# Row maxima of neighbouring PSUM banks taken in pairs by VectorE, in the attention stage of a fused cross-attention and expert kernel

## The chip, the cores and the metric

One core of a Trainium2 chip runs the whole program. The metric is the device time of one execution in microseconds (us). The engines are TensorE (PE in the profile, with its weight loads as PEld), VectorE (DVE), ScalarE (ACT), GpSimd (POOL) and the DMA queues, most of them fed by SyncE (SP). PSUM has eight banks; a bank holds 512 fp32 numbers in each of 128 partitions.

## The reference, cut to what matters

```python
# B=4, S=512, D=256, 16 heads of 16; ctx has the shape of x
q = split(layernorm(x) @ Wq + bq); k = split(ctx @ Wk + bk); v = split(ctx @ Wv + bv)
scores = einsum('bhqd,bhkd->bhqk', q, k) / sqrt(16)
p = softmax(scores, axis=-1)
x = x + einsum('bhqk,bhkd->bhqd', p, v).merge_heads() @ Wo + bo
y = layernorm(x); yn = rmsnorm(y) * norm_w
sim = per head and half: (yn @ wq) . keys            # 8 heads, 2 halves, 64 keys
s1, s2 = top 16 of each half; choose the top 16 of the 256 sums
hidden = gelu(yn . expert_down[chosen]) * relu(score)
x = x + sum(hidden * expert_up[chosen])
```

Softmax subtracts the largest score of a row (one query of one head). Finding these largest scores is what the change touches.

## The kernel before

The attention runs in 16 **groups** of four heads (`NG = 16`, four groups for each of the four batch entries). A group has 16 **blocks** (steps `i = 0..15`): head `i // 4` of the group, and 128 queries `i % 4`, against all 512 keys. Block number `n = 16 g + i` runs through all groups.

The scores are computed twice. `scores(g, i)` (line 1501) multiplies a block with the queries in the partitions into bank `n % 3`, one of **three** banks; VectorE reduces it to one negated maximum for each query (line 1293). When a group's 16 blocks are reduced, `max_parts(g)` (lines 1102 to 1106) splits the maxima into two bf16 parts, TensorE turns them (event "max" at step 3 of the next group), ScalarE copies them out, and SyncE relays them through DRAM into two extra rows of the group's query tile. Two groups later `turned_scores(g, i)` (line 1511) multiplies the same scores turned, with the maxima already subtracted by the two extra rows, into bank 3 or 4; ScalarE exponentiates them (`probabilities`, line 984), and `values` multiplies four blocks of them with the values (four fp32 matmuls into bank 5, at steps 1, 5, 9 and 13).

So in the slot of group g, TensorE does for each step i, in this order: the planned events of the step (transposes and projections for other parts of the program, all through banks 6 and 7), the turned scores of group g - 2, the scores of group g, and at `i % 4 == 1` the values. The order on every engine is fixed by these loops; engines meet at semaphores:

```python
if n >= 3:
    pe.wait_ge(s_max, n - 2)        # scores: block n-3 is reduced
if n >= 2:
    pe.wait_ge(p_ready, n - 1)      # turned scores: its bank is exponentiated
dve.wait_ge(s_full, n + 1)          # reduction: block n is multiplied
```

VectorE's loop has, for each step: at step 0 `max_parts` of the last group, then the reduction of the step, then whatever else is placed there: `first_norm` at step 3 and `first_norm_apply` at step 8 (first group of a batch entry), `normalise` at step 4, residual and second norm at steps 12 to 15 of every fourth group, and from group 8 on the **tasks** of the expert choice (`choose_experts`): 17 tasks for each tile of 128 tokens, spread over two groups from step 5 of the even one. A task is a search (8 top-8 steps and their bookkeeping), a choice, the making of keys or an extraction, of one to three microseconds. In even groups from 8 on, TensorE has two events "sim" at steps 2 and 6, fp32 matmuls of 512 columns.

After the attention, from about 440 us, the experts' stage follows, in which nothing is changed.

## Time and profile before

| | |
|---|---|
| median of 3 runs | 1168.51 us (1166.11 to 1168.63) |
| the profiled execution | 1168.72 us |
| its span, first to last instruction | 1166.9 us |
| TensorE busy | 1032.4 us (88%) |
| VectorE busy | 943.8 us (81%) |
| ScalarE busy | 393.6 us (34%) |
| GpSimd busy | 636.7 us (55%) |
| mean granted TensorE clock | 0.942 of full speed |

Busy shares are means over stages with different limits, so they don't say which engine sets the time of one stage; the views by stretch do. An engine's busy time counts the duration of its instructions, and on VectorE an instruction may start a little before the duration of the one ahead has ended. Several instructions of one line in a row are merged into one row of the timeline (x4). A matmul's end is modelled. In the rows, `mem` is the one SBUF tensor that holds all tiles, and `bank` a PSUM bank.

### The profile page before, as it was taken

To read this page: it belongs to the slowest core of one execution; us is meant where nothing else is said; L and a number is where in the kernel's file an instruction comes from. 1 tells how busy PE (TensorE), PEld (TensorE's weight loads), DVE (VectorE), ACT (ScalarE), POOL (GpSimd) and SP (SyncE) were. 2 spreads that over 40 slices of the span, in tenths; PEclk is the share of its full clock that TensorE was granted. 3 is DMA by queue.
4 is the path that set the end of the run, shared out by engine and by line. 5 is a ranking of instruction groups with operands and counts; after the bars stand their busy time and mean duration, and the time that the engine had idled before them with its cause. 6 is when DMAs were issued, how large, how long until landed. Compare 5 with 4: busy or idle time off the path is not lost.

```text
span 1166.9 us, 28159 instructions
## 1 busy us (share of the span) xinstructions
PE 1032.4 (88%) x10088; PEld 722.1 (62%) x10088; DVE 943.8 (81%) x4847; ACT 393.6 (34%) x725; POOL 636.7 (55%) x793
## 2 busy tenths in 40 slices
PE   5899989876778686598989989999999999999998
PEld 3434444233213224577878778887888878888887
DVE  3676557989998999899999899999989999943210
ACT  2266645443444362232222222222222222222211
POOL 6330510532122225686787777878877787776511
PEclk9799989998969798699999999999999999999999
DMA  7534324222111103700000000000000000000000
GB/s 204 141 131 135 111 74 141 65 92 87 52 51 43 51 7 108 280 3 12 17 21 21 22 21 17 27 11 27 27 15 22 22 17 25 27 31 2 2 19 10
DMA packets 60347, 63.82 MB, mean 55 GB/s; under 512 B 7184, under 2 KB 56592, under 8 KB 59696
## 3 DMA queue, kind: packets, MB, share of 16 engines
q1 hardware_dynamic: 59728, 61.63, 16.6%
q8 instruction: 80, 1.31, 0.5%
q10 hardware_dynamic: 480, 0.39, 0.2%
q14 instruction: 59, 0.48, 0.1%
HBM read 42.34 MB, written 19.66 MB: 53 GB/s over the span
## 4 chain that ended last, share of the span: by engine, by line
PE 42%; DVE 33%; POOL 11%; issue 7%; ACT 2%; DMA 2%; SPq 1%; ACTq 0%; DVEq 0%; POOLq 0%
PE bank L1383 39%; POOL mem L863 4%; DVE mem L1293 4%; DVE mem L1338 4%; PE bank L1386 3%; DVE mem L1229 3%; DVE mem L1176 2%; DVE mem L1175 2%; DVE mem L1225 2%; DVE mem L1232 2%; DVE mem L1212 1%; DVE mem L1335 1%; POOL mem L724 1%; POOL mem L870 1%; DVE mem L1180 1%
## 5 line engine op out<-in xcount | busy, mean ns | idle before, releaser
L1383 PE MATMUL bank<-mem 128*128 128x32 bf16 (+6 forms) x9608 | 984.2, 275 | 93.8 <-DVE mem L1293 34.5
L1383 PEld LDWEIGHTS bank<-mem 128*128 128x128 bf16 (+4 forms) x9608 | 669.8, 122 | 363.0 <-issue 161.4
L863 POOL TENSOR_TENSOR mem<-mem 128x1536 bf16<-128x1536 bf16 x123 | 340.8, 2772 | 138.3 <-DVE mem L1335 138.1
L1293 DVE TENSOR_REDUCE mem<-bank 128x1 f32<-128x512 f32 x256 | 167.8, 682 | 59.8 <-PE bank L1383 58.9
L984 ACT ACTIVATE mem<-bank 128x512 f32<-128x512 f32 x256 | 147.8, 602 | 183.8 <-PE bank L1383 183.0
L1338 DVE TENSOR_TENSOR mem<-mem,bank 128x2048 bf16<-128x2048 bf16 x128 | 155.3, 1213 | 0.0
L1040 ACT COPY mem<-bank 128x512 f32<-128x512 f32 x128 | 75.1, 586 | 113.9 <-PE bank L1383 113.9
L870 POOL TENSOR_TENSOR mem<-mem 128x512 f32<-128x512 f32 x64 | 83.3, 1302 | 50.5 <-ACT mem L1029 50.5
L1386 PE MATMUL bank<-mem 128*128 128x128 f32 (+3 forms) x480 | 74.7, 287 | 37.4 <-DVE mem L1093 11.4
L1386 PEld LDWEIGHTS bank<-mem 128*128 128x128 f32 (+3 forms) x480 | 55.1, 141 | 78.2 <-issue 46.1
L724 POOL TENSOR_TENSOR mem<-mem 128x32 f32<-128x32 f32 (+5 forms) x224 | 45.8, 244 | 97.5 <-DVE mem L1184 97.5
L1031 ACT ACTIVATE bank<-bank 128x512 f32<-128x512 f32 x64 | 37.2, 582 | 171.3 <-PE bank L1383 171.3
L1029 ACT ACTIVATE mem<-bank 128x512 f32<-128x512 f32 x64 | 38.3, 599 | 161.3 <-PE bank L1383 161.3
L1335 DVE TENSOR_TENSOR mem<-mem,bank 128x512 bf16<-128x512 bf16 x128 | 52.3, 409 | 47.6 <-PE bank L1383 44.2
L1352 DVE TENSOR_TENSOR mem<-bank,mem 128x512 f32<-128x512 f32 x64 | 43.8, 684 | 47.0 <-ACT bank L1031 39.0
L1175 DVE FIND_INDEX8 mem<-mem 128x8 uint32<-128x64 f32 x256 | 52.9, 219 | 0.0
L1176 DVE MATCH_REPLACE8 mem<-mem 128x64 f32<-128x64 f32 x256 | 51.6, 209 | 0.0
L745 POOL TENSOR_TENSOR mem<-mem 128x128 f32<-128x128 f32 x16 | 7.2, 451 | 72.8 <-DVE mem L1246 72.8
L1229 DVE MATCH_REPLACE8 mem<-mem 128x50 f32<-128x50 f32 x256 | 46.9, 194 | 0.0
L1180 DVE MAX8 mem<-mem 128x8 f32<-128x64 f32 x256 | 44.2, 215 | 0.0
L1172 DVE MAX8 mem<-mem 128x8 f32<-128x64 f32 x256 | 43.5, 211 | 0.0
L759 POOL TENSOR_SCALAR mem<-mem 128x4 f32<-128x4 f32 x4 | 0.9, 237 | 65.4 <-DVE mem L1085 65.3
(105 smaller groups left out, 770.5 us busy)
## 6 DMA issues: line engine op xcount, KB each, us to landing
mem<-parts_d SPq DMA_DIRECT2D x186, 64.0 KB, 2.3
parts_d<-mem SPq DMA_DIRECT2D x16, 384.0 KB, 3.0
mem<-in_L_ffn_expert_down SPq DMA_DIRECT2D x16, 256.0 KB, 2.8
downT_d<-mem SPq DMA_DIRECT2D x16, 256.0 KB, 3.0
mem<-downT_d SPq DMA_DIRECT2D x4, 1024.0 KB, 7.9
mem<-in_L_ffn_expert_up SPq DMA_DIRECT2D x4, 1024.0 KB, 10.9
tok_d<-mem SPq DMA_DIRECT2D x16, 160.0 KB, 1.8
mem<-tok_d SPq DMA_DIRECT2D x16, 160.0 KB, 2.4
```

The costliest lines, as they stand in the source:

```text
L863: nc.gpsimd.tensor_tensor(ow[q % 2], i0, i1, ALU.mult).then_inc(ow_rdy, 1)
L870: nc.gpsimd.tensor_tensor(gm[q % 4], gm[q % 4], coef[par][:, 2 * q:2 * q + 2, :], ALU.mult)\
L984: nc.scalar.activation(p_sb[quad % 3][:, hh, :], psum[3 + n % 2][:, :], ACT.Exp, scale=DK ** -0.5)\
L1040: nc.scalar.copy(coef[1 - par][:, :, q * TK:(q + 1) * TK], src).then_inc(c_ev, 1)
L1175: steps.count(nc.vector.max_index(i[:, h, c, 0:8], s[:, h, c, 0:8], src[c]))
L1176: cut = [steps.count(nc.vector.match_replace(left[c], s[:, h, c, 0:8], src[c], GONE)) for c in range(2)]
L1229: b.append(steps.count(nc.vector.match_replace(k[:, h, :], o[:, h, 0:8], k[:, h, :], 0.0)))
L1293: nc.vector.tensor_reduce(nmx[g % 2][:, i % TB, i // TB:i // TB + 1], psum[n % 3][:, :], AX.X, ALU.max, negate=True).then_inc(s_max, 1)
L1335: nc.vector.tensor_tensor(oj[q % 2], low.to_broadcast([P, TP, JL, PAIR]), numbers[:, 0:JL, :].unsqueeze(1).to_broadcast([P, TP, JL, PAIR]) ...
L1338: nc.vector.tensor_tensor(oh[q % 2], high.to_broadcast([P, TP, P, PAIR]), numbers.unsqueeze(1).to_broadcast([P, TP, P, PAIR]), ALU.is_equa ...
L1383: return nc.tensor.matmul(o, l, r, start=first, stop=last)
L1386: return nc.tensor.transpose(o, i, ident)
```

## The change

The three banks of the scores become one PSUM tensor of three banks, `bank012`, so that one instruction can read two neighbouring ones. `neighbours(g)` decides for each group which steps are reduced together: two blocks in banks 0 and 1, or in banks 1 and 2 where a group begins at bank 1, and never across the end of a group. A pair is reduced by one instruction at the step of its second block, after the wait for that block, and raises `s_max` by two when it ends. Blocks in bank 2, and those left over, are reduced alone as before. A group that begins at bank 1 has six pairs and four single blocks, any other five pairs and six single blocks. The maxima in `nmx` now lie head by head, as the blocks come, and `max_parts` reads them turned round. TensorE's, ScalarE's and the queues' code is the same.

```diff
-        psum = [ctx.enter_context(nc.psum_tensor(f"bank{i}", [P, 512], F32)) for i in range(8)]
+        three = ctx.enter_context(nc.psum_tensor("bank012", [P, 3 * 512], F32)).rearrange("p (i t) -> p i t", i=3)
+        psum = [three[:, i, :] for i in range(3)]
+        psum += [ctx.enter_context(nc.psum_tensor(f"bank{i}", [P, 512], F32)) for i in range(3, 8)]
...
-        nmx = [mem.take(TB * HG).rearrange("p (t h) -> p t h", t=TB) for _ in range(2)]
+        nmx = [mem.take(HG * TB) for _ in range(2)]
...
+        def neighbours(g):
+
+            last, i = {}, 0
+            while i < 16:
+                blocks = 2 if (16 * g + i) % 3 < 2 and i < 15 else 1
+                i += blocks
+                last[i - 1] = blocks
+            return last
+
+        reduced = [neighbours(g) for g in range(NG)]
...
-                m, n = mpart[g % 2], nmx[g % 2]
+                m, n = mpart[g % 2], nmx[g % 2].rearrange("p (h t) -> p t h", h=HG)
...
-                    if g < NG:
-                        n = 16 * g + i
+                    if g < NG and i in reduced[g]:
+                        n, blocks = 16 * g + i, reduced[g][i]
                         dve.wait_ge(s_full, n + 1)
-                        nc.vector.tensor_reduce(nmx[g % 2][:, i % TB, i // TB:i // TB + 1], psum[n % 3][:, :], AX.X,
-                                                ALU.max, negate=True).then_inc(s_max, 1)
+                        nc.vector.tensor_reduce(nmx[g % 2][:, i + 1 - blocks:i + 1], three[:, n % 3 + 1 - blocks:n % 3 + 1, :],
+                                                AX.X, ALU.max, negate=True).then_inc(s_max, blocks)
```

What stands in a row on an engine is shown at two stretches of the program. The first is group 4, which begins at bank 1. On VectorE before, from block 3 of the group to block 8 (BN_STATS and BN_AGGR are `first_norm`, RECIPROCAL and TENSOR_TENSOR `normalise`):

```order
L1293 TENSOR_REDUCE mem<-bank1 128x1 [waits s_full]
L1080 BN_STATS mem<-mem 128x6 [waits x_ld2]
L1080 BN_STATS mem<-mem 128x6 x3
L1085 BN_AGGR mem<-mem 128x2 [waits ln_stat,ln_rstd]
L1085 BN_AGGR mem<-mem 128x2 [waits ln_stat] x3
L1293 TENSOR_REDUCE mem<-bank2 128x1 [waits s_full]
L1116 RECIPROCAL mem<-bank7 128x16 [waits misc_read1,misc_full1]
L1120 TENSOR_TENSOR mem<-bank7,mem 128x4x64 [waits nrm]
L1293 TENSOR_REDUCE mem<-bank0 128x1 [waits s_full]
L1293 TENSOR_REDUCE mem<-bank1 128x1 [waits s_full]
L1293 TENSOR_REDUCE mem<-bank2 128x1 [waits s_full]
L1293 TENSOR_REDUCE mem<-bank0 128x1 [waits s_full]
```

On VectorE now, from the pairs of blocks 0, 1 and 2, 3 to block 7 (`128x2` is a pair) and `first_norm_apply` (TENSOR_SCALAR):

```order
L1306 TENSOR_REDUCE mem<-bank012 128x2 [waits s_full] x2
L1093 BN_STATS mem<-mem 128x6 [waits x_ld2]
L1093 BN_STATS mem<-mem 128x6 x3
L1098 BN_AGGR mem<-mem 128x2 [waits ln_stat,ln_rstd]
L1098 BN_AGGR mem<-mem 128x2 [waits ln_stat] x3
L1306 TENSOR_REDUCE mem<-bank012 128x1 [waits s_full]
L1129 RECIPROCAL mem<-bank7 128x16 [waits misc_read1,misc_full1]
L1133 TENSOR_TENSOR mem<-bank7,mem 128x4x64 [waits nrm]
L1306 TENSOR_REDUCE mem<-bank012 128x2 [waits s_full]
L1306 TENSOR_REDUCE mem<-bank012 128x1 [waits s_full]
L1106 TENSOR_SCALAR mem<-mem 128x256 [waits misc_full0,ln_stat,ln_rstd]
L1106 TENSOR_SCALAR mem<-mem 128x256 x3
```

Blocks 2 and 3, 5 and 6, 8 and 9 are one instruction each, at the place of the second; the other work of the steps keeps its place.

On TensorE before, group 4 from step 6 to step 9 (bank 3 or 4 with `p_ready` is a turned score, a wait for `s_max` a score, 128x128 transposes of an event):

```order
L1383 MATMUL bank3<-mem 128x512 [waits p_ready]
L1383 MATMUL bank1<-mem 128x512 [waits s_max]
L1386 MATMUL bank6<-mem 128x128 [waits dn_ld0,misc_read0]
L1386 MATMUL bank6<-mem 128x128 x3
L1383 MATMUL bank4<-mem 128x512 [waits p_ready]
L1383 MATMUL bank2<-mem 128x512 [waits s_max]
L1383 MATMUL bank3<-mem 128x512 [waits p_ready]
L1383 MATMUL bank0<-mem 128x512 [waits s_max]
L1386 MATMUL bank7<-mem 128x128 [waits wq_ld0,misc_read1]
L1386 MATMUL bank7<-mem 128x128 x3
L1383 MATMUL bank4<-mem 128x512 [waits p_ready]
L1383 MATMUL bank1<-mem 128x512 [waits s_max]
```

Nothing moved there; the same rows stand there now, with `bank012` for banks 0 to 2. But the scores of step 8 (the third row that waits for `s_max`) need block 5, which VectorE now reduces together with block 6.

The other stretch is the end of group 13 and the start of group 14. On VectorE before, from block 13 of group 13 (MAX with 128x50, MATCH_REPLACE are an extraction, the rest down to the CAST the decoding of a tile, then `max_parts`):

```order
L1293 TENSOR_REDUCE mem<-bank2 128x1 [waits s_full]
L1293 TENSOR_REDUCE mem<-bank0 128x1 [waits s_full]
L1225 MAX mem<-mem 128x8 x4
L1229 MATCH_REPLACE mem<-mem 128x50 [waits dve_step] x4
L1232 MAX mem<-mem 128x8 [waits dve_step] x4
L1241 TENSOR_SCALAR mem<-mem 128x128 [waits dve_step,misc_full1,wsp]
L1243 TENSOR_SCALAR mem<-mem 128x128
L1244 TENSOR_SCALAR mem<-mem 128x128
L1246 SCALAR_TENSOR_TENSOR mem<-mem 128x128 [waits dve_step]
L1249 CAST mem<-mem 128x128 [waits dve_step]
L1250 CAST mem<-mem 128x128
L1293 TENSOR_REDUCE mem<-bank1 128x1 [waits s_full]
```

On VectorE now, from the single block 13 to the pair of blocks 14 and 15:

```order
L1306 TENSOR_REDUCE mem<-bank012 128x1 [waits s_full]
L1238 MAX mem<-mem 128x8 x4
L1242 MATCH_REPLACE mem<-mem 128x50 [waits dve_step] x4
L1245 MAX mem<-mem 128x8 [waits dve_step] x4
L1254 TENSOR_SCALAR mem<-mem 128x128 [waits dve_step,misc_full1,wsp]
L1256 TENSOR_SCALAR mem<-mem 128x128
L1257 TENSOR_SCALAR mem<-mem 128x128
L1259 SCALAR_TENSOR_TENSOR mem<-mem 128x128 [waits dve_step]
L1262 CAST mem<-mem 128x128 [waits dve_step]
L1263 CAST mem<-mem 128x128
L1306 TENSOR_REDUCE mem<-bank012 128x2 [waits s_full]
```

The reduction of block 14 has moved behind the extraction and the decoding, to that of block 15.

## Rows read from the trace of the kernel before

**Rows 1.** The page's groups, and the line alone with its first and last start

```profile
L1293 DVE TENSOR_REDUCE mem<-bank 128x1 f32<-128x512 f32 x256 | 167.8, 682 | 59.8 <-PE bank L1383 58.9
...
L1293 DVE TENSOR_REDUCE mem<-bank x256: 655/680/693, 31.8 to 412.0; 128x1 f32<-128x512 f32 x128
```

**Rows 2.** Busy us by stretch: columns PE, PEld, DVE, ACT, POOL, clock, DMA

```profile
31.00:76.00 45.00, 41.56 (x183) 20.48 (x183) 34.56 (x69) 19.67 (x38) 18.05 (x22) 0.83 0.46 138
76.00:188.00 112.00, 104.80 (x568) 47.46 (x568) 66.64 (x134) 66.19 (x137) 23.01 (x36) 0.95 0.38 119
188.00:412.00 224.00, 174.18 (x764) 63.54 (x761) 210.85 (x1218) 99.25 (x192) 59.52 (x161) 0.86 0.20 64
```

**Rows 3.** Chain by line, from 76 to 188 us, then from 188 to 412

```profile
by line: PE bank L1383 67.8%; PE bank L1386 12.8%; issue 4.9%; ACT mem L937 1.4%; POOL mem L787 1.3%; POOL mem L795 1.3%; ACT mem L992 1.3%; ACT mem L984 1.2%; DVE mem L1129 1.2%; DVE mem L1133 1.1%; DVE mem L1149 0.9%; ACT mem L915 0.6%; D
...
by line: DVE mem L1293 19.7%; PE bank L1383 15.1%; issue 4.8%; DVE mem L1175 3.6%; DVE mem L1176 3.6%; DVE mem L1229 3.2%; SPq L508 2.8%; PE bank L1386 2.5%; DVE mem L1180 2.4%; DVE mem L1172 2.4%; DVE mem L1184 2.1%; DVE mem L1232 2.0%; DV
```

**Rows 4.** Waits from 76 to 188 us: us in total, times, longest

```profile
DVE mem L1293 <- PE bank L1383: 39.4, 40, 3.0
```

**Rows 5.** Waits from 188 to 412 us

```profile
PE bank L1383 <- DVE mem L1293: 32.0, 27, 2.2
...
DVE mem L1293 <- PE bank L1383: 9.7, 13, 1.9
```

**Rows 6.** Timeline (start, us, what), the relay before group 3

```profile
75.96 0.39 PE L1383 MATMUL bank<-mem 98*128 98x512 bf16 x1 [1.59 <-DMA mem<-mrow_d]
```

**Rows 7.** Timeline, VectorE, a run of reductions and two short ones

```profile
102.82 2.47 DVE L1293 TENSOR_REDUCE mem<-bank 128x1 f32<-128x512 f32 x4
...
184.24 0.17 DVE L1102 CAST mem<-mem 128x16 bf16<-128x16 f32 x1
```

**Rows 8.** Timeline, matmul to reduction, and reduction to matmul

```profile
170.83 0.38 PE L1383 MATMUL bank<-mem 96*128 96x512 bf16 x1
...
171.25 0.69 DVE L1293 TENSOR_REDUCE mem<-bank 128x1 f32<-128x512 f32 x1 [0.96 <-PE bank L1383]
...
268.11 0.68 DVE L1293 TENSOR_REDUCE mem<-bank 128x1 f32<-128x512 f32 x1
...
268.85 0.61 PE L1383 MATMUL bank<-mem 96*128 96x512 bf16 x1 [1.46 <-DVE mem L1293]
```

**Rows 9.** Timeline, late places: reduction of the second block, TensorE two blocks on

```profile
84.67 0.69 DVE L1293 TENSOR_REDUCE mem<-bank 128x1 f32<-128x512 f32 x1 [0.18 <-PE bank L1383]
...
85.34 0.60 PE L1383 MATMUL bank<-mem 98*128 98x512 bf16 x2
...
103.32 0.63 PE L1383 MATMUL bank<-mem 98*128 98x512 bf16 x2
...
183.51 0.69 DVE L1293 TENSOR_REDUCE mem<-bank 128x1 f32<-128x512 f32 x1 [0.58 <-PE bank L1383]
...
183.95 0.61 PE L1383 MATMUL bank<-mem 98*128 98x512 bf16 x2
```

**Rows 10.** Timeline, VectorE and TensorE from group 13 to group 14

```profile
348.64 1.27 DVE L1293 TENSOR_REDUCE mem<-bank 128x1 f32<-128x512 f32 x2
...
352.55 0.68 DVE L1293 TENSOR_REDUCE mem<-bank 128x1 f32<-128x512 f32 x1
...
355.49 0.69 DVE L1293 TENSOR_REDUCE mem<-bank 128x1 f32<-128x512 f32 x1 [0.36 <-PE bank L1383]
...
349.45 6.00 PE L1383 MATMUL bank<-mem 96*128 96x512 bf16 x17 [0.38 <-DVE mem L1293]
...
349.83 1.06 PE L1383 MATMUL bank<-mem 98*128 98x512 bf16 x2
```

**Rows 11.** Timeline, VectorE's waits at three reductions

```profile
187.94 0.69 DVE L1293 TENSOR_REDUCE mem<-bank 128x1 f32<-128x512 f32 x1 [1.92 <-PE bank L1383]
...
365.99 0.69 DVE L1293 TENSOR_REDUCE mem<-bank 128x1 f32<-128x512 f32 x1 [1.20 <-PE bank L1383]
...
254.58 0.69 DVE L1293 TENSOR_REDUCE mem<-bank 128x1 f32<-128x512 f32 x1 [1.20 <-PE bank L1383]
```

## The prediction

> **What bounds the kernel now.** I read the views in the order of the groups above. The page [rows 1] gives the instruction at stake: 256 row-maximum reductions of 0.682 us, 167.8 us of VectorE, with 59.8 us of VectorE idling ahead of them, nearly all spent waiting for TensorE. All lie between 31 and 412 us. The busy time by stretch [rows 2] splits that time in two. From 76 to 188 us (groups 3 to 7 of the 16) TensorE is busy 104.80 of 112 us and VectorE only 66.64: TensorE sets the pace. From 188 to 412 us (groups 8 to 15, with the choice of experts on VectorE) it is the reverse: VectorE 210.85 of 224 us, TensorE 174.18. The chain by line agrees [rows 3]: in the first stretch 67.8% and 12.8% of it are TensorE lines and the reduction is not named; in the second the reduction leads with 19.7%. The waits say what could be gained: in the first stretch VectorE waits 39.4 us for scores [rows 4], so a cheaper reduction buys nothing there; in the second TensorE waits for the reduction (32.0 us in 27 waits) and VectorE for TensorE in only 13 places, 9.7 us [rows 5]. Before 76 us the end of the chain is a relay through DRAM: TensorE starts group 3 at 75.96 us after a wait of 1.59 us for it [rows 6]. After 412 us nothing that the change touches is left, and what is gained or lost by then passes on one to one.
>
> **What the change removes.** By the rule that picks pairs, a group has five or six, 85 in all: 171 instructions instead of 256. Groups 8 to 15 have 42 pairs (two groups of six, six of five), groups 3 to 7 have 27. What a pair saves: four reductions in a row take 2.47 us and the last one of them 0.68, so they start (2.47 - 0.68) / 3 = 0.597 us apart [rows 7]. The time per element I take from two VectorE rows of different length, 16 elements in 0.17 us and 512 in 0.68: 0.51 / 496 = 1.03 ns, 0.53 us for 512. So a pair lasts 0.68 + 0.53 = 1.21 us and the next instruction starts 1.13 us after it, against 1.194 for two: 0.064 us saved. The other bound is the whole fixed part of an instruction's duration, 0.68 - 0.53 = 0.15 us. I take 0.064, since start to start is what a busy engine pays. Where VectorE is the bound that is 42 x 0.064 = 2.7 us **gained**; in groups 3 to 7 nothing is.
> The Trainium skill (VectorE: DVE Perf Modes, section "The TRN2 errata — SBUF-src ops pay a fixed extra latency per instruction") gives 120 cycles fixed for a PSUM source and says that many small tiles pay it each: by that, an estimate from the page, the 42 pairs would save 42 x 0.125 = 5.3 us instead of 2.7, and the sum below would be 2.6 us less. The trace shows such a fixed time in the duration, but not between starts; it is rival C below.
> That the maxima now lie head by head makes the first cast and the subtraction of `max_parts` read with a stride; 16 elements in 0.17 us [rows 7], once a group: nothing, 0.1 us each at most.
>
> **What it adds: a bank comes free later.** TensorE may write scores n+3 only when block n is reduced. With a pair (n, n+1) the bank of n waits for block n+1 to be multiplied, and for 1.21 us instead of 0.68. The links [rows 8]: a reduction starts 0.42 us after its matmul (170.83 to 171.25), and a matmul that waited for a bank starts 0.06 us after the reduction's end (268.11 + 0.68 = 268.79 to 268.85). So a pair whose second block's reduction began at R before lets TensorE write two blocks further on at R + 1.21 + 0.06 at the earliest. Compare with when it did so before [rows 9]: a row "x2" is a turned-score matmul and a score matmul, the score starting 0.38 us before the row's end.
> Group 4, blocks 5 and 6: R = 102.82, because VectorE is kept until then by another task (blocks 5 to 8 are the four in a row of [rows 7]); new release 104.09. Block 8's matmul started at 103.32 + 0.63 - 0.38 = 103.57: 0.53 us late. Blocks 6 and 7 of group 3: 84.67 + 1.27 = 85.94 against 85.34 + 0.60 - 0.38 = 85.56: 0.38 us. Last pair of group 7: 183.51 + 1.27 = 184.78 against 184.18: 0.60 us. What decides is what TensorE has between the second block and the second next: with the values' four fp32 matmuls there, the release is in time; with only transposes or nothing, it is not. Over groups 3 to 7 there are seven late places, the first, the one above and the last shown: two at 0.38 us, four at 0.60, one at 0.53. The other 20 pairs are covered by the values, projections or waits for other buffers. TensorE's stream behind the seven is dense (busy 104.80 of 112 us), and behind the waiting matmul on its queue stand the turned scores, the values and the transposes, so ScalarE's exponentials slip with it. Sum: 0.76 + 2.40 + 0.53 = 3.7 us **lost**. Bounds: 0 if waits for ScalarE absorb it all, 5 if the second bank of a cycle is late too.
> In groups 0 to 2 the same happens, but group 3 waits for the relay [rows 6]; 1.59 us cover it. I cost it at nothing; with that cover used up it is 0.5 us.
>
> **The stretch that VectorE bounds.** There the task of the first block (a search, a choice) now runs before the pair, so the bank of the first block comes free a task and a reduction later. Mostly TensorE has room (it waits 32.0 us there anyway). Not at the start of group 14, the place of the third excerpt. Blocks 13 and 14 of group 13 were reduced back to back from 348.64, the second done at 349.91 [rows 10]; TensorE wrote group 14's block 1 at once (349.83 + 1.06 - 0.63 = 350.26) and then ran its stream of 6.00 us (values, both similarity matmuls) that ends with block 2, for which VectorE waited 0.36 us at 355.49. Now block 14 is reduced with block 15, behind the extraction and the decoding, ending at 352.55 + 0.68 - 0.06 = 353.17; block 1's matmul starts at 353.23 instead of 350.26, and the stream behind it ends 3.0 us later with VectorE idle: **3.0 us lost**. Groups 8, 10 and 12 end in other phases and keep their release.
> Where VectorE waited for the second block of a pair [rows 11], it had done the first in the meantime; now it does both after the wait. Three places: 187.94 (followed by another wait, 0.17 us and dense work: 0.3 us), one in group 12 and 365.99 (0.53 each): 1.4 us lost. The wait of 1.20 us at 254.58 is for the first block of one; now a search of 1.7 us runs in it: 0.9 us gained (0 to 1.20). Sum for this stretch: -2.7 + 3.0 + 1.4 - 0.9 = +0.8; bounds -3.6 (nothing late) and +4.5 (another place like group 14's half as dear).
>
> **Sum.** The profiled execution took 1168.72 us (span 1166.9 and what lies around it), 0.2 over the median of 1168.51. 1168.7 + 3.7 + 0.8 = 1173.2; I forecast **1173.2 us**.
>
> **Rivals.**
> *A, slower still by the clock.* TensorE runs at half clock in stretches: mean 0.95 from 76 to 188 us, 0.86 from 188 to 412 [rows 2]. Seven more gaps could add such stretches. If 0.95 becomes 0.92, the first stretch takes 112 x (0.95 / 0.92 - 1) = 3.7 us more: 1176.9. Against it: the gaps are only 0.4 to 0.6 us, and the mean in the second stretch, where TensorE already waits in 27 places and more, is still 0.86.
> The Trainium skill (TensorE: Matmul & The Clock Gate, section "A second HAM failure mode: psum-queue depth-cycling") tells of this very thing, short idles between groups of matmuls that cycle through PSUM making the clock fall and rise; the means of the two stretches are in line with it, but do not show the cause.
> *B, absorbed.* TensorE also waits for ScalarE; if those waits swallow the seven stalls: 1168.7 + 0.8 = 1169.5, no change. Against it: in the two rows of [rows 9] TensorE goes on without a gap.
> *C, the whole fixed part is saved.* 0.15 instead of 0.064 us in 42 pairs is 3.6 us more: 1173.2 - 3.6 = 1169.6, no change. For it: nothing but the durations.
> *D, the other side: three banks are deep enough everywhere.* VectorE paces the scores in all groups, TensorE catches up within a group, and every pair pays out: 85 x 0.064 = 5.4 us, 1163.3. It decides if TensorE has 0.6 us to spare behind each late bank; 104.80 busy of 112 us speaks against it.
> That the pairs are not formed is ruled out by the excerpts.
>
> **How the numbers follow.** Forecast (1171 to 1175.5) 0.50; A 0.22; B 0.12; C 0.08; D 0.08. Slower by over 0.2% (2.3 us, about what a measurement of this kernel can tell from no change): forecast and A, 0.72. Within: B and C, 0.20. Faster: D, 0.08. The range, 1169.0 to 1179.0, takes in A, B and C but not D nor A's far end.
>
> **What would show it.** In the changed kernel's profile: 85 rows of about 1.21 us with two outputs and 86 of 0.68; VectorE's busy time less by 85 x 0.15 = 13 us of row time though little is gained; group 8's first maxima about 3.7 us later than before, each late place a wait of TensorE for the reduction just before a score matmul; from there to the last maximum (412.0 before) another 0.8 us, with one VectorE wait of over 3 us early in group 14 and the idle time at 254.58 gone; the time after the last maximum unchanged. I am wrong if a pair is much shorter than 1.21 us, if the first stretch does not lengthen, or if the granted clock in either stretch moves by more than 0.02.

## The result, and the profile after

| | before | after |
|---|---|---|
| median | 1168.63 us (5 runs, 1166.11 to 1170.39) | 1177.14 us (5 runs, 1176.61 to 1181.81) |
| ratio, 95% interval | | 1.0086 (1.0062 to 1.0111) |
| the profiled execution, its span | 1168.72, 1166.9 us | 1176.61, 1174.8 us |
| VectorE busy, its instructions | 943.8 us, 4847 | 938.2 us, 4762 |
| TensorE busy | 1032.4 us | 1030.0 us |
| mean granted TensorE clock | 0.942 | 0.944 |

Slower by 0.86% by the ratio of the runs (the two medians differ by 8.5 us, 0.73%); the forecast was slower, by 0.4% (1173.2 us), the range 1169.0 to 1179.0. VectorE has 85 instructions fewer and 5.6 us less to do, and the kernel takes 8.5 us more at the medians.

The reduction in the profile after: the page's row of the line, and the line by shape. It answers to [rows 1]:

```profile
L1306 DVE TENSOR_REDUCE mem<-bank 128x1 f32<-128x512 f32 (+1 forms) x171 | 159.0, 948 | 74.7 <-PE bank L1396 74.6
...
L1306 DVE TENSOR_REDUCE mem<-bank 128x2 f32<-128x1024 f32 x85 | 103.6, 1218 | 66.3 <-PE bank L1396 66.3
L1306 DVE TENSOR_REDUCE mem<-bank 128x1 f32<-128x512 f32 x86 | 58.5, 681 | 8.4 <-PE bank L1396 8.3
```

85 pairs of 1.218 us and 86 singles of 0.681. The idle time ahead of the reductions rose from 59.8 to 74.7 us, and nearly all of it now stands ahead of pairs, since a pair waits for its second block.

The busy time of the two stretches, each taken to the same point of the program as in [rows 2] (columns as there):

```profile
76.00:191.00 115.00, 104.00 (x570) 47.98 (x568) 65.56 (x111) 67.40 (x139) 23.01 (x36) 0.99 0.37 117
191.00:421.00 230.00, 174.31 (x762) 64.28 (x760) 209.12 (x1178) 99.21 (x191) 59.90 (x162) 0.86 0.20 62
```

The first stretch is 3 us longer with 104.00 us of TensorE's work as before, although its clock was even higher (0.99 against 0.95); the second is 6 us longer. The waits for the reduction in the two, which answer to [rows 4, 5]:

```profile
DVE mem L1306 <- PE bank L1396: 44.8, 30, 3.7
...
PE bank L1396 <- DVE mem L1306: 4.7, 10, 0.9
...
PE bank L1396 <- DVE mem L1306: 42.7, 31, 4.9
...
DVE mem L1306 <- PE bank L1396: 18.2, 13, 5.4
```

In the first stretch TensorE's matmuls waited for the reduction in 10 places, 4.7 us; before, in 2, 1.4 us. In the second they waited 42.7 us instead of 32.0, and VectorE for TensorE 18.2 us instead of 9.7, **in 13 places again**. One of those is 5.41 us long; it is the start of group 14:

```profile
350.91 0.67 DVE L1306 TENSOR_REDUCE mem<-bank 128x1 f32<-128x512 f32 x1
...
354.22 1.22 DVE L1306 TENSOR_REDUCE mem<-bank 128x2 f32<-128x1024 f32 x1
...
362.29 1.82 DVE L1306 TENSOR_REDUCE mem<-bank 128x2 f32<-128x1024 f32 x2 [5.41 <-PE bank L1396]
...
355.49 6.69 PE L1396 MATMUL bank<-mem 96*128 96x512 bf16 x15 [3.17 <-DVE mem L1306]
```

These are rows of VectorE's and, the last one, of TensorE's timeline; they answer to [rows 10]. The single block 13 of group 13 is reduced at 350.91. Block 14 could be, too, but stands with block 15 at 354.22, behind the extraction and the decoding. TensorE waits 3.17 us for its bank, runs the stream of values and similarities that was 4.8 us long before and is 6.3 now, and VectorE waits 5.41 us for the block at its end.

To compare runs, I use **slots**: the time from the first instruction of `max_parts` for one group (the cast, L1102, L1115 or L1117) to that of the next, so the slot of group g is that in which its own scores are reduced. The slot of group 14 before, and after:

```profile
353.26 0.27 DVE L1102 CAST mem<-mem 128x16 bf16<-128x16 f32 x1
...
385.53 0.17 DVE L1102 CAST mem<-mem 128x16 bf16<-128x16 f32 x1
```

```profile
355.47 0.17 DVE L1115 CAST mem<-mem 128x16 bf16<-128x16 f32 x1
...
393.91 0.17 DVE L1115 CAST mem<-mem 128x16 bf16<-128x16 f32 x1
```

385.53 - 353.26 = 32.3 us before, 393.91 - 355.47 = 38.4 us after. All slots that matter, taken in the same way from each trace (group 10 stands apart, see below; "to the end" is from the last cast to the last turned score matmul):

| kernel | groups 1 to 7 | 8 | 9 | 10 | 11 | 12 | 13 | 14 | 15 | to the end |
|---|---|---|---|---|---|---|---|---|---|---|
| before | 136.4 | 27.9 | 28.9 | 33.1 | 27.2 | 24.7 | 27.2 | 32.3 | 27.2 | 25.7 |
| after | 139.6 | 28.3 | 28.3 | 32.6 | 26.9 | 25.4 | 27.0 | 38.4 | 27.4 | 24.3 |

Two numbers carry the result: +3.2 us up to group 7, and +6.1 in the slot of group 14. The rest of groups 8 to 15 with the end is 1.7 us **shorter** than before, but 1.4 us of that lies behind the last cast, where nothing is reduced any more. The busy time of that stretch before, and after, columns as in [rows 2]:

```profile
412.70:438.50 25.80, 20.83 (x106) 5.78 (x106) 23.41 (x197) 17.30 (x33) 6.98 (x27) 0.93 0.02 8
```

```profile
421.30:445.70 24.40, 19.38 (x107) 5.51 (x106) 22.39 (x191) 18.09 (x34) 6.93 (x27) 1.00 0.03 8
```

TensorE needs 19.38 instead of 20.83 us there, at a granted clock of 1.00 instead of 0.93. The slots of groups 8 to 13 and 15 together are only 0.3 us shorter.

### The profile page after: what moved, and what is told of

It is laid out like the page before. It is cut to its first block, busy times and chain, and to the rows that moved or that the text cites. A ratio compares the mean times of both kernels' runs of the same rounds, so it can differ in the third digit from the quotient of the medians.

```text
span 1174.8 us, 28159 instructions
## 1 busy us (share of the span) xinstructions
PE 1030.0 (88%) x10088; PEld 723.5 (62%) x10088; DVE 938.2 (80%) x4762; ACT 394.1 (34%) x725; POOL 636.8 (54%) x793
## 4 chain that ended last, share of the span: by engine, by line
PE 43%; DVE 34%; POOL 11%; issue 7%; ACT 2%; DMA 2%; SPq 1%; ACTq 0%; DVEq 0%; POOLq 0%
PE bank L1396 40%; DVE mem L1306 5%; DVE mem L1351 4%; POOL mem L876 4%; PE bank L1399 3%; DVE mem L1242 2%; DVE mem L1189 2%; DVE mem L1188 2%; DVE mem L1238 2%; DVE mem L1245 1%; DVE mem L1225 1%; DVE mem L1348 1%; DVE mem L1193 1%; DVE mem L1185 1%; POOL mem L737 1%
## 5 line engine op out<-in xcount | busy, mean ns | idle before, releaser
L1306 DVE TENSOR_REDUCE mem<-bank 128x1 f32<-128x512 f32 (+1 forms) x171 | 159.0, 948 | 74.7 <-PE bank L1396 74.6
```

The source lines that it names most:

```text
L1306: nc.vector.tensor_reduce(nmx[g % 2][:, i + 1 - blocks:i + 1], three[:, n % 3 + 1 - blocks:n % 3 + 1, :], AX.X, ALU.max, negate=True).then ...
```

## The experiments

Theory T: the change costs at few places, where a score bank comes free late and TensorE has nothing else to do; elsewhere it saves a little. Its rivals: E, every pair costs a little (8.5 / 85 = 0.1 us) by the two-bank read itself; A, what is lost in the first stretch is absorbed behind it (this is B of the prediction; the letters here are those of the expectations); K, the granted clock, by which no edit of single pairs would make a definite change. All kernels of a group ran on one chip beside the kernel before, whose median was 1167.24, 1168.5 and 1167.63 us for the three groups.

### Which pairs cost: one undone, those from group 8, those up to group 7

```diff
-                blocks = 2 if (16 * g + i) % 3 < 2 and i < 15 else 1
+                blocks = 2 if (16 * g + i) % 3 < 2 and i < 15 and (g, i) != (13, 14) else 1
```

> The changed kernel with one pair undone: blocks 14 and 15 of group 13 are reduced one by one, block 14 again ahead of the extraction and the decoding; the other 84 pairs stay. Theory T (few late banks): the step from 2.3 to 6.7 us that the traces show at the start of group 14 goes; 4 to 6 us less than the changed kernel, that is 1171 to 1173 us, +0.3% to +0.4% on the kernel before; score matmuls of group 14 from block 2 on are 2 to 3 us later than before instead of 6.7. Rival E (every pair costs about 8 / 85 = 0.1 us, by the two-bank read itself): 0.1 us less, 1177 us. Rival K (the granted clock): no definite change.

```diff
+                blocks = 2 if (16 * g + i) % 3 < 2 and i < 15 and g >= 8 else 1
```

> Pairs only in groups 8 to 15 (42), groups 0 to 7 as before. Theory T: group 8 starts as in the kernel before (within 0.3 us instead of 2.9 later); the rest keeps its loss, so about 3 us less than the changed kernel, 1174 us, with the step at group 14. Rival E: 43 x 0.1 = 4.3 us less, 1173 us, and the delay grows evenly through groups 8 to 15 instead of in steps.

```diff
+                blocks = 2 if (16 * g + i) % 3 < 2 and i < 15 and g < 8 else 1
```

> Pairs only in groups 0 to 7 (43), the rest as before. Theory T: group 8 starts 2.5 to 3.2 us later than in the kernel before, in steps of 0.4 to 1.0 us at single blocks of groups 3 to 7, and that delay is carried to the end: 1171.5 us. Rival E: 1173 us, evenly grown. Rival A (absorbed by what VectorE bounds behind it): less than 1 us at the end, 1169.5.

| pairs | ratio to before, 95% | groups 1 to 7 | 8 | 9 | 10 | 11 | 12 | 13 | 14 | 15 | to the end |
|---|---|---|---|---|---|---|---|---|---|---|---|
| all but one | 1.0051 (1.0032 to 1.0069) | 140.0 | 28.3 | 28.3 | 32.8 | 26.9 | 25.4 | 26.9 | 31.6 | 27.3 | 24.3 |
| from group 8 | 1.0047 (1.0034 to 1.0061) | 136.6 | 28.0 | 29.7 | 35.0 | 26.9 | 25.5 | 27.0 | 36.5 | 27.3 | 24.3 |
| to group 7 | 1.0043 (1.0025 to 1.0061) | 140.2 | 28.0 | 29.2 | 31.8 | 27.2 | 24.7 | 27.2 | 32.0 | 27.4 | 25.5 |

Groups 1 to 7 take 139.6 to 140.2 us with pairs in them and 136.4 to 136.6 without, whatever stands behind. It isn't given back later: with pairs up to group 7 alone the program is 5.0 us slower at the medians, so rival A falls. With one pair of 85 undone, the slot of group 14 falls to 31.6 us, and its block 2 is multiplied 0.06 us after the cast (1.82 before, 6.33 in the changed kernel). So rival E falls: 84 pairs are left and that slot has its old length. Against the kernel before the program is now 0.51% slower instead of 0.86% (0.69% in a repeat below); the intervals of these overlap, and the same pair is tested twice more below. The two halves lose 0.47% and 0.43%, 0.90% together, against 0.86% and 0.69% for the whole; the intervals allow it.

### The order without the merging

```diff
-                        nc.vector.tensor_reduce(nmx[g % 2][:, i + 1 - blocks:i + 1], three[:, n % 3 + 1 - blocks:n % 3 + 1, :],
-                                                AX.X, ALU.max, negate=True).then_inc(s_max, blocks)
+                        for back_by in range(blocks - 1, -1, -1):
+                            nc.vector.tensor_reduce(nmx[g % 2][:, i - back_by:i - back_by + 1], psum[n % 3 - back_by], AX.X,
+                                                    ALU.max, negate=True).then_inc(s_max, 1)
```

> All pairs keep their place in VectorE's order (both reductions at the step of the second block), but are two instructions of one bank each, each raising the semaphore by one. It parts the order from the merging. Theory T: in groups 3 to 7 the first bank comes free 0.5 to 0.6 us earlier than with the merged one, and the late places all but go: group 8 starts within 0.6 us of the kernel before. At the start of group 14 the bank still waits behind the extraction: 3.5 to 5 us lost there. The 42 merged savings of 0.06 us go too (2.7 us). Sum 1168.6 + 0.5 + 2.7 + 5 = 1176.8, 1175 to 1178 us: about the changed kernel's time, but with the loss all behind 188 us. Rival E (the two-bank read costs): about the kernel before, 1168.6 us.

1174.66 us, ratio 1.0058 (1.0039 to 1.0076), so most of the loss is there without a merged instruction. The expected 1176.8 us counts 2.7 us for savings that "go too", but the kernel before, from which that sum starts, never had them; without them it is 1174.1. Its profiled execution was the quickest of its nine (1167.90 us, the others 1170.26 to 1177.35), so its trace tells where single places wait, not what makes up the median: the slot of group 14 is 3.6 us longer in it, the median some 7 us, and the difference stays open. The waits of TensorE's matmuls for the reduction in the first stretch, of this kernel, and of the one with pairs up to group 7 (us, times, longest):

```profile
PE bank L1397 <- DVE mem L1307: 0.9, 2, 0.5
```

```profile
PE bank L1396 <- DVE mem L1306: 4.7, 10, 0.9
```

0.9 us in 2 places against 4.7 in 10: the late places of the first stretch come from the **merging**, since the first of two single reductions frees its bank 0.54 us earlier than a merged one (0.68 against 1.22 us after their start). From group 3's step 4 to group 8's step 1 it takes 102.1 us, as kernels with the old order there do (102.1 to 102.8), against 105.7 to 106.1 with the pairs. The slot of group 14 is 35.9 us here: most of what is lost there comes from the **order**. And this run prices the merged instruction where VectorE is the bound: the slot of group 11 is 27.2 us with single reductions in either order and 26.9 with five pairs: 0.3 / 5 = 0.06 us for a pair.

### One pair alone

```diff
+                blocks = 2 if (g, i) == (13, 14) else 1
```

> The kernel before with a single pair, blocks 14 and 15 of group 13. Theory T: that pair alone makes the score matmul of group 14, block 1, 3.0 us late, and the slot of group 14 (from its maxima's split to the next one's) 35.5 to 37.5 us instead of 32.0 to 32.7; total 3 to 5 us over the kernel before, nothing else moves by more than the clock's phase. Rival E (many pairs each cost a little): 0.1 us, no difference.

1172.42 us, ratio 1.0042 (1.0024 to 1.0060): 4.8 us by **one** merged instruction out of 255. Groups 1 to 7 take 136.4 us as before, groups 8, 9, 11, 12, 13 and 15 are within 0.1 us of before, group 10 is at 33.8 and the end at 25.3; the slot of group 14 is 37.4 us instead of 32.3. Its rows, VectorE and then TensorE:

```profile
348.88 0.68 DVE L1306 TENSOR_REDUCE mem<-bank 128x1 f32<-128x512 f32 x1
...
352.20 1.22 DVE L1306 TENSOR_REDUCE mem<-bank 128x2 f32<-128x1024 f32 x1
...
360.24 0.69 DVE L1306 TENSOR_REDUCE mem<-bank 128x1 f32<-128x512 f32 x1 [4.78 <-PE bank L1396]
...
353.47 6.73 PE L1396 MATMUL bank<-mem 96*128 96x512 bf16 x15 [2.75 <-DVE mem L1306]
```

The same picture with nothing else changed: the pair at 352.20, TensorE 2.75 us idle before block 1's matmul at 353.47, and VectorE 4.78 us idle for the end of the stream. For comparison, the kernel with pairs from group 8 on but without this one (below), where TensorE starts after 0.32 us and the whole run of 17 is 4.25 us long:

```profile
348.90 1.27 DVE L1306 TENSOR_REDUCE mem<-bank 128x1 f32<-128x512 f32 x2
...
352.81 0.68 DVE L1306 TENSOR_REDUCE mem<-bank 128x1 f32<-128x512 f32 x1
...
349.72 4.25 PE L1396 MATMUL bank<-mem 96*128 96x512 bf16 x17 [0.32 <-DVE mem L1306]
```

### Pairs where the wait is covered

In the first stretch: pairs only up to group 7, and only where the values stand between the second block and the matmul that needs the first one's bank.

```diff
+                blocks = 2 if (16 * g + i) % 3 < 2 and i < 15 and g < 8 and i % 4 in (0, 3) else 1
```

> Pairs only in groups 0 to 7 and only where the values' four fp32 matmuls stand on TensorE's queue between the second block and the matmul that waits for the first's bank (the second block's step is 0 or 1 modulo 4): 30 pairs of 43. Theory T: no bank is late; from the score matmul of group 3, step 4, to that of group 8, step 1, 102 to 103 us as before instead of 106, and the total within 0.2% of the kernel before. Rival E (each pair costs by itself): 30 / 43 of the 3.3 us, 2.3 us more.

1168.99 us, ratio 1.0007 (0.9989 to 1.0024). TensorE's wait for the reduction there:

```profile
PE bank L1396 <- DVE mem L1306: 0.5, 1, 0.5
```

One place, 0.5 us, and 102.0 us from group 3's step 4 to group 8's step 1, against 102.1 to 102.8 in kernels without pairs there. Groups 1 to 7 even take 134.7 us in this trace, and 135.4 in that of the two single reductions, where slots 1 to 3 together, with the relay, are shorter; I didn't follow that, and no median shows it. So these pairs cost nothing and, with VectorE not the bound, bring nothing; the others hold the loss of that stretch.

In the second stretch: pairs from group 8 on but for the dear one.

```diff
+                blocks = 2 if (16 * g + i) % 3 < 2 and i < 15 and g >= 8 and (g, i) != (13, 14) else 1
```

> Pairs only in groups 8 to 15, at the step of the second block as in the changed kernel, but blocks 14 and 15 of group 13 apart: 41 pairs. Theory T: no late bank in groups 0 to 7, none at the start of group 14; what is left is the saving of the merged instruction less the waits for second blocks: 1 to 2 us faster than the kernel before, 0.1%. Rival (the release behind a task costs in other places too): 0.2% slower or more.

1168.25 us, ratio 1.0008 (0.9991 to 1.0024): the same as before, not the 1 to 2 us faster that I expected. Its slots from group 8: 28.0, 28.8, 33.7, 26.9, 25.4, 27.0, 31.6, 27.4 and 24.3 to the end, without group 10 219.4 against 221.1 before: 1.7 us gained in the trace, too little for the medians to show. And 1.4 of these stand behind the last cast, at a clock of 1.00 against 0.93 as in the changed kernel; in the slots themselves, group 10 again left out, 41 pairs gained 0.3 us.

### Pairs at the first block's place

If the loss is the bank that waits behind a task, a pair may be reduced at the step of its first block, with the task behind it.

```diff
-            last, i = {}, 0
+            first, i = {}, 0
             while i < 16:
-                blocks = 2 if (16 * g + i) % 3 < 2 and i < 15 else 1
+                blocks = 2 if (16 * g + i) % 3 < 2 and i < 15 and g >= 8 else 1
+                first[i] = blocks
                 i += blocks
-                last[i - 1] = blocks
-            return last
+            return first
...
                         n, blocks = 16 * g + i, reduced[g][i]
-                        dve.wait_ge(s_full, n + 1)
-                        nc.vector.tensor_reduce(nmx[g % 2][:, i + 1 - blocks:i + 1], three[:, n % 3 + 1 - blocks:n % 3 + 1, :],
+                        dve.wait_ge(s_full, n + blocks)
+                        nc.vector.tensor_reduce(nmx[g % 2][:, i:i + blocks], three[:, n % 3:n % 3 + blocks, :],
```

> Pairs only in groups 8 to 15, and reduced at the step of the FIRST block: VectorE waits there for the second block too, and the tasks of the first block run behind the pair instead of ahead of it. Theory T: the first block's bank comes free 0.53 us later than before instead of a task and a reduction later, so the steps at the start of group 14 go. Each pair saves 0.064 us (2.7 us in all), but in 11 of 42 places the second block is not there when VectorE comes to the first, by 0.2 to 2.6 us, 12 us in all, of which it waited about 7 before: 2 to 5 us lost there. Sum: 0 to +2.5 us on the kernel before. Rival (late banks don't matter in this stretch, and the changed kernel lost there by the clock): the same 5.5 us as with pairs at the second block.

And the same with pairs only where, by the trace of before, the second block lay ready at the first one's step, 30 of them:

```diff
+        READY = {8: [7, 10, 13], 9: [0, 9, 12], 10: [0, 12, 14], 11: [1, 4, 7, 10, 13], 12: [0, 9, 12], 13: [0, 2, 5, 8, 11, 14], 14: [10, 13], 15: [0, 3, 7, 9, 12]}
...
-                blocks = 2 if (16 * g + i) % 3 < 2 and i < 15 and g >= 8 else 1
+                blocks = 2 if (16 * g + i) % 3 < 2 and i < 15 and i in READY.get(g, ()) else 1
```

> The same, but only the 30 pairs of groups 8 to 15 whose second block, by the trace of before, is multiplied at least 0.4 us before VectorE comes to the first; all else as in the kernel before. Theory T: 30 x 0.064 = 1.9 us gained, no bank late where it counts: 0.15% faster than the kernel before. If the whole fixed part of 0.15 us were saved: 4.5 us, 0.4% faster. Rival: any two-bank read or any later release costs, 0.2% to 0.4% slower.

1173.9 us, ratio 1.0042 (1.0028 to 1.0055), and 1172.2 us, ratio 1.0025 (1.0012 to 1.0038), where I had expected at most 2.5 us (0.2%) slower for the first and 0.15% faster for the second: two misses, and in the total the first came out about as its rival had it (5.5 us). The slot of group 14 is indeed 32.7 and 31.7 us, so the dear place is gone. But that of group 10 is 36.9 and 36.5, and in the first of the two that of group 12 is 27.0 against 24.7. So I ran the second once more, and the kernel before with it:

> The variant with 30 pairs at the place of their first block once more, for a second trace. Its first trace showed 1.8 us gained outside group 10's slot and 3.4 us lost in it, where TensorE's stream of fp32 matmuls ran at half clock; the unchanged code of groups 8 to 15 took 31.8, 33.1 and 35.7 us there in three traces. Theory P (group 10's slot depends on the phase of the clock, whatever the pairs): the slot is somewhere between 31 and 37 us again, and the total within 0.3% of the kernel before. Theory Q (the early pairs cause it): 36 to 37 us again, and 0.2% to 0.4% slower.

> The kernel before, unchanged, timed against itself, for a second trace of it and for what the comparison makes of no change. Ratio 1.000 within 0.15%. Group 10's slot between 31 and 37 us (33.1 in the first trace); all the others as in the first trace within 0.5 us, but for those in which the granted clock differs.

The early pairs again: ratio 1.0022 (1.0007 to 1.0038), group 10's slot 36.5. The kernel before against itself: 0.9999 (0.9984 to 1.0013), slot 32.8, all other slots within 0.7 us of its first trace. With three traces at 36.5, 36.5 and 36.9 against five in which that stretch is unchanged at 31.8 to 35.7 (33.1, 32.8, 31.8, 33.8 and 35.7), it is likelier that this belongs to the early pairs (theory Q), but the ranges almost meet. What the slot hangs on is TensorE's stream between blocks 1 and 2 of the group. The windows of just that stream, in the kernels with unchanged code there (pairs up to group 7; before again; pairs with the values behind), columns as in [rows 2]:

```profile
241.60:245.80 4.20, 3.35 (x15) 1.13 (x15) 4.06 (x27) 0.60 (x1) 1.55 (x4) 1.00 0.54 170
```

```profile
236.30:241.60 5.30, 4.52 (x15) 1.07 (x14) 4.69 (x26) 0.60 (x1) 3.17 (x8) 0.77 0.47 148
```

```profile
236.20:244.50 8.30, 6.35 (x15) 1.78 (x15) 4.99 (x28) 0.60 (x1) 4.21 (x8) 0.51 0.30 95
```

4.2 us at full clock, 5.3 at 0.77, 8.3 at 0.51, for the same instructions. But the clock is not all of it: TensorE is busy for 3.35, 4.52 and 6.35 us of these windows and waits in the rest, nearly all of it for one transfer, which brings the input of the similarity matmuls. Their rows in the same three kernels:

```profile
243.87 2.39 PE L1396 MATMUL bank<-mem 128*128 128x512 f32 x6 [0.85 <-DMA mem<-xn_d]
```

```profile
239.62 2.39 PE L1383 MATMUL bank<-mem 128*128 128x512 f32 x6 [0.78 <-DMA mem<-xn_d]
```

```profile
240.54 4.61 PE L1396 MATMUL bank<-mem 128*128 128x512 f32 x6 [1.95 <-DMA mem<-xn_d]
```

The six matmuls take 2.39 us at one clock level and 4.61 at the other, and the wait for the transfer is 0.85, 0.78 and 1.95 us. In the kernel with pairs from group 8 on, whose slot is 35.0 us, that wait is 3.39 us. So group 10's slot varies with two things, the clock and when this transfer lands. With the 30 early pairs the stream was 8.2 us long at 0.50 in both traces, 1.73 and 1.74 us of it this wait. In these two, and with all 42 early pairs, TensorE had also waited 1.16 us for the reduction of block 14 of group 9 right ahead of the stream, which it does in no other trace:

```profile
236.57 2.48 PE L1398 MATMUL bank<-mem 96*128 96x512 bf16 x9 [1.16 <-DVE mem L1308]
```

That doesn't show the cause, for the kernel with pairs only where the values stand behind them had the same clock there without that wait. Why the clock stood at its lower level each time is open; no run took it apart.

### The changed kernel again

> The changed kernel once more, beside the others on one chip, for a second trace of it. Theory T: 0.6% to 0.9% slower than the kernel before; from the score matmul of group 3, step 4, to that of group 8, step 1, 3.3 us more than before (102.8), and from there to the last turned score 3 to 5 us more. If the second number is below 1 or above 7 this time, it belongs to the phase of the clock in one execution and not to the change.

1176.39 us, ratio 1.0069 (1.0050 to 1.0089). Its profiled execution was the quickest of four (1172.11, the others 1176.07 to 1177.99). Groups 1 to 7 139.7 us, group 14's slot 36.6, group 10's 31.3; from group 3's step 4 to group 8's step 1 105.7 us against 102.8 before. So the two places of the loss are the same ones again. But the other half of the expectation missed: from group 8's step 1 to the last turned score I had expected 3 to 5 us more than before, and it is 255.2 against 254.2 us, 1.0 more (4.3 more in the first trace, 258.5). Group 14's slot is 4.3 us longer than before, group 10's 1.8 shorter and the end 1.4 shorter: in a single trace the clock and the transfer at those other places can hide most of the pair's loss. The medians don't rest on one execution.

## Why the prediction was right, and where it was not

**Right in sign and in the two places, short in size.** The time is in the range, 4 us above the forecast, and the loss is nearly twice the one forecast (8.5 us at the medians, against 4.5). That it lies beside rival A's 1176.9 us is chance, as the clock of the first stretch did not fall. Step by step:

*The price of a pair.* Forecast 1.21 us, measured 1.218; the next instruction starts 1.14 us behind one (99.96 to 101.10 in the trace after), forecast 1.13. The saving of 0.064 us for each pair is what group 11's slot shows (0.06). Rival C, the whole fixed part, is out, and with it the reading of the Trainium skill's figure (VectorE: DVE Perf Modes, section "The TRN2 errata — SBUF-src ops pay a fixed extra latency per instruction") as time that comes back for every instruction saved. In durations it does come back: 256 x 0.682 = 174.6 us before, 58.5 + 103.6 = 162.1 after, 12.5 us less (forecast 13). But durations of neighbours overlap: the page books only 167.8 - 159.0 = 8.8 us less for the line, and between starts it is 85 x 0.06 = 5.

*Late banks in the first stretch.* Forecast 3.7 us in seven places, with 0 as a bound; measured 3.2 us over groups 1 to 7 between the two profiled executions, and over all traces 105.7 to 106.1 us against 102.1 to 102.8 from group 3's step 4 to group 8's step 1, 3.5 us between the middles. That it comes so close is partly luck, since two misses cancel. The seven places are those in which the score matmuls' starts fall behind before, by 0.45, 0.69, 1.04, 0.68, 0.69, 0.46 and 0.69, which is 0.07 to 0.09 more than forecast in six of them, 4.7 us in all; 1.3 to 1.5 us came back in waits for others at the start of group 7, and the other shifts (-0.2, -0.3, and +0.8 then -0.4 in group 6) cancel. The worked example, blocks 5 and 6 of group 4, was the one that I had wrong, 1.04 instead of 0.53:

```profile
99.96 1.22 DVE L1306 TENSOR_REDUCE mem<-bank 128x2 f32<-128x1024 f32 x1 [1.08 <-PE bank L1396]
...
102.69 0.66 DVE L1306 TENSOR_REDUCE mem<-bank 128x1 f32<-128x512 f32 x1
...
103.89 1.81 DVE L1306 TENSOR_REDUCE mem<-bank 128x2 f32<-128x1024 f32 x2
...
105.16 0.39 PE L1396 MATMUL bank<-mem 96*128 96x512 bf16 x1 [0.90 <-DVE mem L1306]
```

VectorE, VectorE, TensorE. The pair of blocks 2 and 3 ran 1.22 us from 99.96, after waiting 1.08 us for block 3; before, block 2 had been done by then. So VectorE came to `first_norm`, block 4 (102.69) and this pair (103.89) half a microsecond late by itself, and TensorE waited 0.90 us for this pair. I had seen that a pair does both reductions after a wait, but charged it only in the second stretch.

*Group 14.* Forecast 3.0 us, measured 4.2 to 6.1 in the slot (36.5, 36.6, 37.4 and 38.4 us with the pair, 32.0 to 32.4 in the four traces with unchanged code there). **This is the term that was mis-sized.** The release itself was 3.0 us late as worked out: block 1's matmul began 3.0 us before the cast in the kernels with the old order there (3.3 where only this pair was undone) and together with it in those with the pair. But I took TensorE's stream behind it as unchanged at 4.8 us. Its windows in the kernel with the dear pair apart, before, and after:

```profile
350.20:353.60 3.40, 3.40 (x16) 1.08 (x15) 3.23 (x24) 0.60 (x1) 0.81 (x2) 1.00 0.00 0
```

```profile
350.30:355.10 4.80, 4.80 (x16) 1.28 (x14) 4.56 (x25) 0.60 (x1) 2.28 (x6) 0.67 0.00 0
```

```profile
355.50:361.80 6.30, 6.30 (x14) 1.78 (x15) 1.31 (x4) 0.00 (x0) 1.21 (x4) 0.51 0.00 0
```

3.4 us at full clock, 4.8 at 0.67, 6.3 at 0.51, for the same matmuls. I had read the 6.00 us of [rows 10] as the stream's length when it was already a length at a mixed clock, and with 3 us of idle time ahead of it TensorE ran it at half clock throughout in two of the four traces with the pair (6.3 and 6.4 us; 4.9 and 5.1 in the others). That is 1.5 us more in the profiled execution. The rest, 1.7 us, came behind block 2's matmul, from which it is 32.1 us to the end of the slot against 30.4 to 30.5 in the traces with unchanged code. It is 31.5 us in the four traces that have the pairs of group 14 and no stream at half clock throughout (two with the dear pair, two without it), so 1.0 to 1.1 us of this belong to those other pairs: in the second trace of the changed kernel the reductions fall behind by 0.6 us at blocks 7 and 8, which the forecast had charged with 0.53 us at 365.99, and by 0.5 us at blocks 13 and 14, which it had not. With the dear pair alone, and the stream at half clock, it is 31.0 us, 0.6 us for the clock. The dear pair by itself made the slot 5.1 us longer in that trace.

*The rest of the second stretch.* Forecast -2.7 + 1.4 - 0.9 = -2.2 us; measured -1.7 in the changed kernel and -1.7 in the one without the dear pair. **Near in sum, but by luck:** 1.4 of the 1.7 us stand behind the last cast, where the prediction had said that nothing changes, with the clock at 1.00 instead of 0.93. In the slots of groups 8 to 13 and 15, where most of the 2.2 us were to be gained, it is 0.3 us. The 0.53 us of group 12 and the wait filled in group 10 were not measured one by one; group 12's slot is 0.7 us longer, group 9's 0.6 shorter.

*Groups 0 to 2.* I costed them at nothing, since group 3 waits for the relay. Slots 1 and 2 are 1.4 and 0.8 us longer with the pairs (15.1 and 14.5 against 13.7 and 13.7), and most of it is given back at the relay: from the first score to group 3's step 4 it is 49.8 to 51.7 us in four traces with the pairs (mean 50.9) and 50.2 to 50.6 in those without. That is the 0 to 0.5 us that I had set as bounds.

*Rivals.* Of those in the prediction, A was half right: no lasting change of the mean clock (0.944 against 0.942), but half clock in the stream of group 14 in two of four executions. A sign of being wrong that I had set did come out: the clock of the first stretch moved by more than 0.02, from 0.95 to 0.99. It moved up, though (the second trace of the kernel before has 0.97 there), so it took nothing from the loss and may have hidden some of it. B (absorbed) and D (every pair pays out) are out.

*What adds up:* 3.2 + 6.1 - 1.7 = 7.6 of the 7.9 us between the two spans. Forecast 3.7 + 3.0 - 2.2 = 4.5.

None of the variants beat the kernel before by more than its measurement can tell. Pairs with the values behind them and the 41 pairs from group 8 on cost nothing and gained nothing that shows.

## What to carry to other kernels

Merging two small instructions into one moves the first to the place of the second and lets its buffer go only when both are done; before counting what is saved, look for who waits for that buffer, and for what long task now stands ahead of it. What is saved is read from the distance between starts of neighbouring instructions, not from their durations. One place may hold half of the loss: find it by the slot times of two traces, and test it by making that one place alone. Before a difference between two traces is put down to a change, look at the granted clock and at the waits for transfers in the same stretch.

## What the runs showed that I had not expected

The length of one and the same stream of matmuls (bf16 scores, four fp32 products of 512 columns and fp32 similarities) was 3.4, 4.8 to 5.1 and 6.3 to 6.4 us in group 14 and, with 0.8 to 2.0 us of waiting for a transfer in it, 4.2, 5.3 and 8.3 us in group 10, with the granted clock at 1.00 (2.4 GHz), at 0.64 to 0.77 (a mean over both levels) and at 0.50 to 0.51 (1.2 GHz). The wait ahead of the stream doesn't settle which it is. In group 14 the clock was 1.00 when TensorE had waited 0.32 us before the stream, but 0.67 in the kernel before, with 0.38 us; it was 0.50 and 0.51 in two executions with 2.75 and 3.17 us, but 0.65 and 0.64 in two others with 2.76 and 2.75. This, at two or three places in an execution, may be a part of why executions of the kernel before lie between 1163.19 and 1172.54 us, and why the interval of a ratio is 0.13% to 0.18% wide to either side with 12 executions: 0.25% could be told from none, 0.08% could not. The ten waits in the first stretch, the longest of 0.9 us, went with a mean clock of 0.99. The Trainium skill (TensorE: Matmul & The Clock Gate, section "A second HAM failure mode: psum-queue depth-cycling") puts such swings down to short idles between bursts that cycle through PSUM; the ten short waits of that stretch did not bring them about.
